# One sort key: VectorE forms the negated row maxima of a head group before the low part of a later group's queries

## The chip, the cores and the metric

One core of a Trainium2 chip. The metric is the device time of one execution in microseconds (us), as the median of several runs; less is better. Five engines work side by side: TensorE (PE, with its weight loads as PEld), VectorE (DVE), ScalarE (ACT), GpSimd (POOL) and SyncE (SP), which here only issues transfers. Each runs its own list of instructions in order and meets the others through semaphores.

## What is computed

An attention block (8 sequences of 512 tokens, 256 channels, 16 heads, latent width 32), a layer norm of input plus attention, a soft mixture of 16 experts, and a last layer norm. Only the attention matters here:

```
q_lat = rope(q @ q2l_w.T + q2l_b)      k_lat = rope(k @ kv2l_w.T + kv2l_b)
q_for_k = q_lat @ wqk_w.T + wqk_b
att = softmax(causal(q_for_k @ k_lat.T * 32 ** -0.5))
y = (att @ v_lat) @ l2o_w.T + l2o_b
```

## The kernel before

**Groups.** The 16 heads of a sequence are taken in four groups of four, so there are 32 groups over the 8 sequences; they are numbered 0 to 31 here (group 4b + g is group g of sequence b). The score matrix of a group is computed twice. A first pass of six "max" units (matmul lines 1461 and 1464) is reduced by VectorE to row maxima `mx` (line 1171). The negated maxima then become two more rows of the query operand `qks`, so that the second pass, six "exp" units (line 1477), comes out of TensorE already shifted and ScalarE only takes the exponential (line 874). GpSimd sets the causal part to zero (line 724, the "mask" steps) and TensorE multiplies with the values (line 1488).

**From maxima to rows (steps `negmax` and `neg`).** VectorE forms -mx in two small `scalar_tensor_tensor` instructions of 128x16: line 1179 writes the high part from `mx` and `zeros`, line 1181 the rest from `mx` and the high part, after a semaphore wait on the first. TensorE transposes the pair into the PSUM bank `misc` (line 1469), ScalarE copies it out (line 864) and a transfer on ScalarE's queue places it in `qks` (line 869).

**Queries (steps `wqk`, `qhi`, `qlo`, `stack`).** Two groups ahead, TensorE writes a group's queries into the same bank `misc` (line 1448). ScalarE rounds them to the high part (line 852) and VectorE forms the low part (line 1165, in from PSUM and from SBUF, 128x512). That instruction also hands `misc` back (`misc_drained`), and SyncE then issues twelve transfers that stack the group's operands in `qks` (line 411) for its max units.

```
elif name == "qlo":
    g = st[2]
    dve.wait_ge(q_high, group(b, g))
    nc.vector.scalar_tensor_tensor(out=stg[g % 2][:, 0, :], in0=misc[:, :], scalar=bwq[:, 0:1],
                                   in1=fp(stg[g % 2][:, 1, :]), op0=ALU.add, op1=ALU.subtract).then_inc(misc_drained, 1)
...
elif name in MISC_STEPS:
    pe.wait_ge(misc_drained, misc_count(st, 0))
...
elif name == "neg":
    g = st[2]
    pe.wait_ge(neg_ready, group(b, g))
```

TensorE's `misc` users follow one another in the order in which TensorE has them: queries of group n+2 (`wqk`), maxima of group n (`neg`), a transpose of outputs (`yT`). So the transpose of group n's maxima waits for two things of VectorE: the maxima themselves (`neg_ready`, line 1181) and the bank, which the low query part of group n+2 (line 1165) gives back.

**Rotary products.** GpSimd multiplies the rotated latents of a coming group by the sine (line 704, both inputs in SBUF, 128x1024) and adds the cosine product of VectorE (line 1161) to it (line 710).

**Order.** `order()` gives each step of an engine a time: 8 slots per group plus the offset of its kind in `PE_AT`, `DVE_AT` and so on (single steps of the first sequence have fixed times in `DVE_EARLY` and its likes), and sorts by it. In `DVE_AT`, `qlo` of group n+2 stands at 8(n+2) - 10.0 = 8n + 6.0, `negmax` of group n at 8n + 6.05, the first max unit of group n+1 at 8n + 4.89 and the second at 8n + 6.22.

Of the kernel before, what the change touches and what calls it, by code (L numbers as in the profile page):

```python
# [40 lines left out]

PE_AT = {"lat": -20.25, "wqk": -9.25, "max": 0.0, "neg": 11.0, "exp": 13.25, "v": 14.55, "pv": 15.75, "yT": 28.75, "yTT": 53.5, "cproj": 58.5, "wv": -10.384, "seT": 5.624}
ACT_AT = {"stack": -9.0, "xth": -30.5, "lat": -22.0, "khi": -12.85, "qhi": -9.58, "neg": 9.57, "exp": 11.74, "y": 22.25, "yTT": 52.85, "apply": 76.25, "wlat": -30.402, "senorm": -2.024, "seT": 7, "seh": 9.429}
DVE_AT = {"xtl": -32.0, "blat": -28.9, "kvrows": -28.8, "slotg": -28.781, "shuffle": -21.3, "cos": -17.25, "qlo": -10.0, "max": -3.11, "negmax": 6.05, "v": 11.5, "yT": 26.15, "cproj": 55.1, "ln": 56.75, "wlat": -30.314, "wv": -17.071, "sestat": -23.24, "sescale": -7.5, "sel": 9.985}
POOL_AT = {"sin": -26.06, "add": -23.69, "klo": -21.92, "mask": 2.69, "bias": 42.5}
SP_AT = {"xt": -52.5, "x": 28.5, "stack": -22.15, "store": 83.25}

# [111 lines left out]
def block_kernel(nc, a, out):  # L159
# [316 lines left out]
    with nc.Block() as block:  # L476
# [550 lines left out]
        def _(dve):  # L1027
# [46 lines left out]

            for st in order(DVE_AT, DVE_FRONT, DVE_LAST, DVE_JOIN, DVE_EARLY):
                name, b = st[:2]
# [623 lines left out]
```

## Time and profile before

| what | value |
|---|---|
| median of 3 runs | 1191.9 us (1191.51 to 1192.89) |
| profiled execution | 1193.62 us, of which the profile's span is 1191.9 us |
| mean granted clock of TensorE | 0.983 of full speed |
| busy, share of the span | PE 95%, PEld 76%, DVE 65%, ACT 56%, POOL 49% |
| chain that ended last, by engine | PE 83%, DVE 8%, ACT 5%, issue 2% |

The attention fills the span up to about 525 us. Busy time is the time in which an engine's instructions run; for TensorE they overlap, since they are pipelined. The chain that ended last is followed back from the last instruction, at each step to what released it. In a timeline, an instruction that waits inside the engine counts as running.

### The profile page before, as it was taken

What the parts mean: (1) busy time and instruction counts of PE and PEld (TensorE: products, weight loads), DVE (VectorE), ACT (ScalarE), POOL (GpSimd) and SP (SyncE); (2) the same over time, 40 slices, a digit from 0 to 9 for tenths busy, and PEclk for the clock granted to TensorE, in tenths of its full rate; (3) what the DMA queues carried; (4) which work ended last, traced back from release to release, by engine and by line L of the source; (5) the groups of instructions that cost most, each with busy time, mean ns of one, the idle gap of its engine ahead of it and who ended that gap; (6) DMA issues with size and microseconds to landing.
All of it is one profiled execution on the core that took longest, in us unless ns stands there. A gap on an engine that the chain in (4) does not pass through costs nothing.

```text
span 1191.9 us, 19111 instructions
## 1 busy us (share of the span) xinstructions
PE 1137.4 (95%) x6849; PEld 904.1 (76%) x6882; DVE 772.6 (65%) x1251; ACT 670.3 (56%) x946; POOL 579.4 (49%) x399
## 2 busy tenths in 40 slices
PE   7799999999999999997999999979999999999996
PEld 5566767676767667665888888858888888888885
DVE  6878787879696978656677777635455454523344
ACT  2555565665666565656797777745556555530112
POOL 5555565556556555421666666664444544430000
PEclk9899999999999999989999999999999999999998
DMA  4645454645455655611144335365555445365661
GB/s 150 146 106 140 114 124 107 162 113 155 114 157 123 160 126 127 171 61 53 60 160 159 125 124 185 100 202 176 167 179 185 146 152 165 115 216 170 242 224 54
DMA packets 126670, 170.29 MB, mean 143 GB/s; under 512 B 47041, under 2 KB 77186, under 8 KB 126594
## 3 DMA queue, kind: packets, MB, share of 16 engines
q1 hardware_dynamic: 124018, 167.95, 48.4%
q10 hardware_dynamic: 2576, 1.35, 0.5%
q8 instruction: 45, 0.74, 0.3%
q14 instruction: 31, 0.25, 0.1%
HBM read 72.26 MB, written 37.75 MB: 92 GB/s over the span
## 4 chain that ended last, share of the span: by engine, by line
PE 83%; DVE 8%; ACT 5%; issue 2%; POOL 1%; DMA 1%; SPq 1%; ACTq 0%; DVEq 0%; POOLq 0%
PE ring L456 12%; PE ring L457 11%; PE ring L458 11%; PE ring L1627 7%; PE tail L1488 6%; PE ring L1477 5%; PE ring L1461 4%; PE tail L456 4%; PE tail L458 4%; PE tail L457 4%; ACT pt L874 3%; PE ring L1510 2%; PE tail L1627 2%; PE tail L1448 2%; PE ring L1564 2%
## 5 line engine op out<-in xcount | busy, mean ns | idle before, releaser
L1171 DVE TENSOR_REDUCE mx<-ring 128x4 f32<-128x512 f32 (+2 forms) x192 | 199.7, 1042 | 72.8 <-PE ring L1464 55.5
L874 ACT ACTIVATE pt<-ring 128x1024 f32<-128x1024 f32 (+1 forms) x192 | 169.0, 881 | 91.6 <-PE ring L1477 87.6
L724 POOL TENSOR_SCALAR_AFFINE_SELECT pt<-pt 128x512 f32<-128x512 f32 x128 | 81.4, 636 | 187.9 <-ACT pt L874 187.9
L1477 PE MATMUL ring<-qks 98*128 98x256 f32 (+3 forms) x512 | 136.7, 370 | 4.5 <-DVE mx L1171 2.0
L1461 PE MATMUL ring<-qks 96*128 96x384 f32 (+3 forms) x512 | 120.1, 337 | 5.3 <-DMA qks<-stg 4.1
L741 POOL TENSOR_TENSOR dl<-e,dh 128x1024 fp32r<-128x1024 f32 x32 | 76.5, 2403 | 94.3 <-ACT e L945 94.3
L765 POOL TENSOR_TENSOR hl<-hid,hh 128x512 fp32r<-128x512 f32 x64 | 82.7, 1303 | 76.9 <-ACT hh L980 76.9
L1477 PEld LDWEIGHTS ring<-qks 98*128 98x128 f32 x512 | 79.3, 191 | 32.2 <-issue 20.5
L1289 DVE SCALAR_TENSOR_TENSOR hid<-ring,bias_e,gate 128x512 f32<-128x512 f32 x64 | 47.9, 748 | 81.1 <-ACT gate L974 49.5
L1461 PEld LDWEIGHTS ring<-qks 96*128 96x128 f32 x512 | 80.8, 193 | 20.5 <-issue 5.9
L710 POOL TENSOR_TENSOR rope<-rope,rot 128x1024 f32<-128x1024 f32 x31 | 75.1, 2421 | 36.5 <-DVE rope L1161 36.5
L1627 PE MATMUL ring<-eo,c 128*128 (+1 forms) x384 | 88.3, 379 | 0.0
L1488 PE MATMUL tail<-pt,va 128*32 128x512 f32 (+3 forms) x1024 | 83.0, 440 | 0.0
L974 ACT ACTIVATE gate<-ring,bias_e 128x512 f32<-128x512 f32 x64 | 44.1, 689 | 67.4 <-PE ring L458 61.4
L1627 PEld LDWEIGHTS ring<-eo,c 128*128 128x128 f32 x384 | 72.9, 190 | 9.9
L757 POOL TENSOR_TENSOR wul<-wu,wuh 128x1024 fp32r<-128x1024 f32 x16 | 42.5, 2657 | 76.0 <-ACT wuh L799 76.0
L1014 ACT ACTIVATE y<-y,nmr,r 128x256 f32<-128x256 f32 x32 | 16.7, 590 | 104.6 <-DVE nmr L1354 104.6
L704 POOL TENSOR_TENSOR rot<-rot,sin 128x1024 f32<-128x1024 f32 x31 | 73.8, 2382 | 1.3 <-DVE rot L1145 1.1
L817 ACT ACTIVATE lat<-ring,blat 128x512 f32<-128x512 f32 x32 | 22.1, 690 | 90.9 <-PE ring L458 73.1
L980 ACT ACTIVATE hh<-hid 128x512 fp32r<-128x512 f32 x64 | 40.2, 628 | 58.2 <-PE tail L458 49.2
L456 PE MATMUL tail<-wdh,hh 128*128 128x256 f32 x240 | 67.9, 283 | 0.5 <-POOL hl L765 0.5
L458 PE MATMUL tail<-wdl,hh 128*128 128x256 f32 x240 | 67.9, 283 | 0.0
(247 smaller groups left out, 3071.6 us busy)
## 6 DMA issues: line engine op xcount, KB each, us to landing
qks<-stg SPq DMA_DIRECT2D x378, 128.0 KB, 2.5
c_dram<-c2s SPq DMA_DIRECT2D x32, 512.0 KB, 5.0
c<-c_dram SPq DMA_DIRECT2D x32, 512.0 KB, 6.6
sl_dram<-sls SPq DMA_DIRECT2D x32, 256.0 KB, 3.4
wg<-in_wg SPq DMA_DIRECT2D x16, 512.0 KB, 5.4
wu<-in_wu SPq DMA_DIRECT2D x16, 512.0 KB, 6.3
wd<-in_wd SPq DMA_DIRECT2D x16, 512.0 KB, 7.1
sl<-sl_dram SPq DMA_DIRECT2D x16, 512.0 KB, 4.5
```

The lines of the kernel that those rows point to most:

```text
L456: nc.tensor.matmul(dst, lh, rh, start=first, stop=False)
L457: nc.tensor.matmul(dst, ll, rh, start=False, stop=False)
L458: return nc.tensor.matmul(dst, lh, rl, start=False, stop=last)
L724: nc.gpsimd.affine_select(out=m, in_=m, compare_op=ALU.is_ge, fill=0.0, base=0, pattern=[[0, GH], [1, P]], channel_multiplier=-1).then_inc ...
L741: nc.gpsimd.tensor_tensor(out=dl[h][:, rows, :], in0=e2[u][:, :, :], in1=fp(dh[h][:, rows, :]), op=ALU.subtract).then_inc(d_low, 1)
L765: nc.gpsimd.tensor_tensor(out=hl[:, f, :], in0=hid[f % 2][:, :], in1=fp(hh[:, f, :]), op=ALU.subtract).then_inc(hid_low, 1)
L874: nc.scalar.activation(pt[j][:, h:h + heads, 0:n], heads_of(tile, heads, n), ACT.Exp, scale=SCALE).then_inc(empty, 1)
L1171: nc.vector.tensor_reduce(out=mx[:, g, h:h + heads, i], in_=heads_of(tile, heads, (i + 1) * P), axis=AX.X, op=ALU.max).then_inc(empty, 1)
L1461: nc.tensor.matmul(scores[:, h, :], qks[0:KS_ROWS, g, 0, h0 + h, i * P:(i + 1) * P], qks[0:KS_ROWS, g, 1, h0 + h, 0:n], start=(h % some == ...
L1477: last = nc.tensor.matmul(scores[:, h, :], qks[0:KS_ROWS + 2, g, 1, h0 + h, j * P:(j + 1) * P], qks[0:KS_ROWS + 2, g, 0, h0 + h, j * P:T], ...
L1488: last = nc.tensor.matmul(ybank[h * L:(h + 1) * L, j * P:T], va[:, j, g * GH + h, :], pt[j][:, h, 0:T - j * P], start=(j == 0), stop=(j == ...
L1627: last = nc.tensor.matmul(acc[i][t // 2][:, t % 2, 0:DO], c2[i][:, n, t * P:(t + 1) * P], eo[:, n, b, :], start=(n == 0), stop=(n == NS - 1))
```

## The change

VectorE's offset for `qlo` goes from -10.0 to -9.9. The low query part of group n+2 then has the time 8n + 6.1 and stands behind the negated maxima of group n (8n + 6.05) and still ahead of the second max unit of group n+1 (8n + 6.22). No other step lies between, and no other engine's order changes. The steps of groups 0 to 2 have fixed times, so 29 pairs of neighbours are swapped: maxima of groups 1 to 29, low query parts of groups 3 to 31.

```
-DVE_AT = {... "cos": -17.25, "qlo": -10.0, "max": -3.11, "negmax": 6.05, ...
+DVE_AT = {... "cos": -17.25, "qlo": -9.9, "max": -3.11, "negmax": 6.05, ...
```

## Rows read from the trace of the kernel before

**Rows 1.** Stretches: us, busy per engine (instructions), TensorE clock, DMA share, GB/s.

```profile
281.00:343.00 62.00, 61.18 (x420) 43.33 (x424) 50.97 (x82) 38.76 (x59) 36.30 (x29) 1.00 0.55 137
```

**Rows 2.** Timeline, all engines, around group 17: start us, length us, engine, line.

```profile
308.17 2.38 POOL L704 TENSOR_TENSOR rot<-rot,sin 128x1024 f32<-128x1024 f32 x1
...
308.90 0.69 DVE L1171 TENSOR_REDUCE mx<-ring 128x4 f32<-128x512 f32 x1 [0.54 <-remote]
308.99 0.68 ACT L852 ACTIVATE stg<-tail,bwq 128x512 fp32r<-128x512 f32 x1
...
309.70 0.75 DVE L1165 SCALAR_TENSOR_TENSOR stg<-tail,bwq,stg 128x512 fp32r<-128x512 f32 x1
...
310.37 0.22 DVE L1179 SCALAR_TENSOR_TENSOR negmax<-mx,zeros 128x16 fp32r<-128x16 f32 x1
...
310.51 0.63 POOL L724 TENSOR_SCALAR_AFFINE_SELECT pt<-pt 128x512 f32<-128x512 f32 x1
...
310.62 0.55 DVE L1181 SCALAR_TENSOR_TENSOR negmax<-mx,negmax 128x16 fp32r<-128x16 f32 x1
...
310.88 0.28 PE L1464 MATMUL ring<-maskb,identb 128*128 128x128 bf16 x2
311.10 1.21 DVE L1171 TENSOR_REDUCE mx<-ring 128x4 f32<-128x1024 f32 x1
...
311.32 0.27 PE L1469 MATMUL tail<-ident,negmax 128*32 128x128 f32 x1 [0.15 <-DVE negmax L1181]
```

**Rows 3.** TensorE's waits, whole execution: who waited for whom, us, times, longest.

```profile
PE tail L1469 <- DVE negmax L1181: 3.9, 22, 0.4
```

**Rows 4.** Timeline around group 0, where no query part precedes the maxima.

```profile
49.73 2.38 POOL L704 TENSOR_TENSOR rot<-rot,sin 128x1024 f32<-128x1024 f32 x1
...
51.28 0.85 DVE L1179 SCALAR_TENSOR_TENSOR negmax<-mx,zeros 128x16 fp32r<-128x16 f32 x1
...
52.17 0.17 DVE L1181 SCALAR_TENSOR_TENSOR negmax<-mx,negmax 128x16 fp32r<-128x16 f32 x1
...
52.49 0.27 PE L1469 MATMUL tail<-ident,negmax 128*32 128x128 f32 x1 [0.40 <-DVE negmax L1181]
```

**Rows 5.** Timeline around group 30, whose maxima no query part precedes either.

```profile
507.09 0.17 DVE L1179 SCALAR_TENSOR_TENSOR negmax<-mx,zeros 128x16 fp32r<-128x16 f32 x1
...
507.29 0.17 DVE L1181 SCALAR_TENSOR_TENSOR negmax<-mx,negmax 128x16 fp32r<-128x16 f32 x1
...
508.06 0.64 POOL L724 TENSOR_SCALAR_AFFINE_SELECT pt<-pt 128x512 f32<-128x512 f32 x1 [3.51 <-ACT pt L874]
```

**Rows 6.** The low query part over the whole execution: ns min/median/max.

```profile
L1165 DVE SCALAR_TENSOR_TENSOR stg<-tail,bwq,stg x32: 722/751/760, 25.8 to 493.8; 128x512 fp32r<-128x512 f32 x32
```

**Rows 7.** Timeline around group 6, third of its sequence.

```profile
139.45 0.55 DVE L1181 SCALAR_TENSOR_TENSOR negmax<-mx,negmax 128x16 fp32r<-128x16 f32 x1
...
143.06 0.29 PE L1464 MATMUL ring<-maskb,identb 128*128 128x128 bf16 x2
143.19 0.27 PE L1469 MATMUL tail<-ident,negmax 128*32 128x128 f32 x1
...
144.60 2.39 POOL L710 TENSOR_TENSOR rope<-rope,rot 128x1024 f32<-128x1024 f32 x1
...
146.27 0.74 DVE L1208 TENSOR_SCALAR nv<-meanvar 128x4 f32<-128x4 f32 x1
```

**Rows 8.** Timeline around group 1, TensorE.

```profile
67.33 0.29 PE L1464 MATMUL ring<-maskb,identb 128*128 128x128 bf16 x2
...
67.77 0.27 PE L1469 MATMUL tail<-ident,negmax 128*32 128x128 f32 x1
```

**Rows 9.** Timeline, stacking of group 5 and its first max unit.

```profile
94.01 8.88 SPq L411 DMA_DIRECT2D qks<-stg  x12
...
105.32 0.56 PE L1461 MATMUL ring<-qks 96*128 96x128 f32 x4
```

**Rows 10.** Page, DMA issues: count, KB each, median us from issue to landing.

```profile
qks<-stg SPq DMA_DIRECT2D x378, 128.0 KB, 2.5
```

## What the change will do, foretold from the trace of before

> **What bounds the kernel now.** I read the stretches first, to see whether the attention is bound by one engine; then the waits of TensorE; then the timeline of one group; then the same instructions in groups where something around them differs.
>
> Over one sequence in the steady part TensorE is busy for 61.18 of 62 us at full granted clock, VectorE for 51 [rows 1]. So whatever keeps TensorE idle there is added to the time, and little idle time is left in which a new stall could be given back. The waits of TensorE name the place of the change: the transpose of the negated maxima waited 22 times for line 1181, 3.9 us in all [rows 3]. One of the 22 is group 0, with 0.40 us [rows 4], whose order the change leaves alone. So 21 of the 29 swapped groups have VectorE's maxima on the path. The other eight are groups 6, 10, 14, 18, 22 and 26, where TensorE comes to the transpose 3.2 us after the maxima are there (139.45 + 0.55 = 140.00 against 143.19, [rows 7]), and groups 1 and 29, where line 1181 ends just as TensorE gets there.
>
> In group 17 VectorE does: max unit (to 309.59), low query part 309.70 to 310.45, line 1179 310.37 to 310.59, line 1181 310.62 to 311.17, next max unit; the transpose starts 0.15 later, at 311.32 [rows 2]. What the reader is to see is the length of the two small instructions. Both handle 128x16, yet take 0.22 and 0.55 us. In group 30 they take 0.17 each [rows 5]. The difference is GpSimd: in group 17 line 1179 ends 0.04 us after GpSimd's sine product (308.17 + 2.38 = 310.55), line 1181 0.03 us after GpSimd's mask (310.51 + 0.63 = 311.14) [rows 2]; in group 30 GpSimd does nothing until 508.06 [rows 5]. Groups 2 to 28 all show the pattern of group 17, 27 times over. Group 0 is the test, since it has no query part in front of the maxima: line 1179 begins while the sine product runs, takes 0.85 us and ends at 52.13, 0.02 after the product (49.73 + 2.38 = 52.11); line 1181, with no mask behind the product, takes 0.17 [rows 4]. So a small instruction with both inputs in SBUF stands still until the GpSimd instruction under way ends, whenever it came. The low query part, one input of which is in PSUM, takes 722 to 760 ns in all 32 groups [rows 6], the sine product beside it or not.
>
> **The change part by part.** It adds and removes no instruction; 29 times it exchanges 0.75 us of work with a pair of small instructions.
>
> The maxima first. Each instruction of VectorE starts 0.07 to 0.08 us before the end of the one in front (310.37 against 310.45, [rows 2]). Behind the max unit, line 1179 would start so at 309.51 in group 17. The sine product runs until 310.55, so line 1179 ends at 310.59 as before, now after 1.08 us instead of 0.22. The mask follows the product as before, so line 1181 ends at 311.17 as before. The maxima gain nothing.
>
> The query part next. ScalarE's high part is there at 309.67 (308.99 + 0.68, [rows 2]), so nothing but VectorE's order holds line 1165. It starts 0.07 before line 1181's end, as the next max unit did (311.10 against 311.17), and ends at 311.10 + 0.75 = 311.85. In effect the query part used to run in the shadow of the sine product, and the shadow is now spent on waiting.
>
> The transpose waits for the bank as well as for the maxima, so its releaser becomes line 1165: 311.85 + 0.15 = 312.00 instead of 311.32, 0.67 to 0.68 us more. I take 0.67. On VectorE the next max unit and the cosine product are queued behind; they move by the same 0.67, and TensorE, which has to drain them later, has moved with them. TensorE, ScalarE and GpSimd then go on from the transpose as before, all shifted, and the next group repeats it: the phase between the sine product, which hangs on an exponential and so on TensorE, and the max unit stays.
>
> Bounds for a group: below, the pair of small instructions costs 0.37 us from first start to last end, as in group 30 (507.09 to 507.46, [rows 5]); then the query part ends at 309.51 + 0.37 - 0.07 + 0.75 = 310.56, the transpose is released at 310.71, and TensorE, which without a wait starts it 0.13 after line 1464 (143.06 and 143.19, [rows 7]), goes at 310.88 + 0.13 = 311.01, a gain of 0.31. Above, both wait in full: 0.67. I take the upper end, because group 0 is the changed order with the sine product running [rows 4].
>
> The Trainium skill, "VectorE: DVE Perf Modes", section on the TRN2 errata, gives an fp32 two-input instruction of N elements (N + 151) / 0.96 ns, an estimate of 0.174 us for 16 elements: the 0.17 of group 30 agrees, the 0.22 and 0.55 of group 17 don't. By that figure alone the sum would be a gain of about 7 us. The Trainium skill, "SBUF — State Buffer", section "Who interferes with whom", says that a VectorE instruction with two SBUF inputs and a GpSimd instruction that reads SBUF exclude each other, the later one waiting for the earlier one's end: by that rule the sum is the loss below, and groups 0 and 17 agree with it.
>
> The other eight swapped groups. Six don't wait at the transpose. There VectorE runs late instead, by at most 0.67, until line 1208 in the layer norm, which already takes 0.74 us and ends at 147.01, with GpSimd's addition (144.60 + 2.39 = 146.99, [rows 7]): the lag ends in that wait, so 0; without that cover six such lags would reach TensorE, at most 6 x 0.44 = 2.6 us (0.67 less some 0.2 that VectorE idles ahead of the layer norm). In groups 1 and 29 no sine product is running when line 1179 comes. There the transpose gains 67.77 - (67.33 + 0.13) = 0.31 each [rows 8]. Together -0.6.
>
> The stacking. Its twelve transfers follow line 1165, so they start 1.40 us later, of which TensorE's own shift takes back 0.67. The tightest place is group 5's stack: the last of twelve issues starts about 0.6 us before 94.01 + 8.88 = 102.89, lands about 2.5 us later [rows 10], so near 104.8, and its first max unit runs at 105.32 [rows 9]. A slack of 0.5 against 0.73: at most 0.2 us, once. Elsewhere it is 1.3 us or more. I cost it at nothing.
>
> Sum: 21 x 0.67 = 14.1, less 0.6, is +13.5 us. On the profiled execution (1193.62 us, of which 1191.9 in the span) that is 1207.1; on the median of the runs shown, 1191.9, it is 1205.4.
>
> **The rivals.**
> *Nothing holds the maxima* (0.07). If line 1179 doesn't wait for a product that was running long before, 21 + 2 groups gain 0.31: -7.1 us, 1184.8. It decides if line 1179 takes about 0.2 us in groups 2 to 28. Group 0 speaks against it.
> *Half of the wait* (0.09). Line 1179, ready early, is through at the product's end and line 1181 gets ahead of the mask (310.62 to 310.79): the query part ends at 310.72 + 0.75 = 311.47, the transpose starts at 311.62, +0.30 in 21 groups, less 0.6: +5.7, 1197.6. Against it: in group 17 line 1179 was already waiting at the product's end, and the mask still went first [rows 2].
> *Given back* (0.05). TensorE has 62 - 61.18 = 0.8 us idle per sequence [rows 1], and seven sequences of it would not cover 13.5 us. Still, if the lists absorb the shift, it is within 0.2%, 1191 to 1193.
> *More than the sum* (0.05). Lags in the six groups and a late stack: 13.5 + 2.6 + 0.2, 1208.2.
> The forecast holds 0.74, with its own range of 1203.5 to 1207.
>
> **How the numbers follow.** 0.2% of the time, 2.4 us, is about what a measurement can tell from no change. Faster 0.07, same 0.05, slower 0.74 + 0.09 + 0.05 = 0.88. The range runs from below the half wait (1197) to the sum with all lags (1208.5) and leaves out the first and third rival, 0.12.
>
> **What the profile of the changed kernel would show.** Line 1179 at about 1.1 us instead of 0.23 in groups 2 to 28, ending with the sine product; line 1181 still 0.55, ending with the mask; line 1165 behind them at 0.75; the transpose waiting for line 1165 and no longer for line 1181, idle about 0.67 us more each time; the steady sequence 62.0 + 3 x 0.67 = 64.0 us long. The prediction is wrong if line 1179 comes out short, if the mask falls behind line 1181, or if the sequence is longer by less than 2 us.

## The result, and the profile of the changed kernel

The changed kernel takes 1201.64 us (median of 6 runs, 1200.84 to 1204.66) against 1191.57 us of the kernel before (6 runs, 1189.51 to 1192.89). The ratio is 1.0085, with a 95% interval of 1.0072 to 1.0098: slower by 10.1 us, 8.6 to 11.7. The forecast was 1205.4 us, in a range of 1197.0 to 1208.5. Direction and mechanism were right; the size came out 3.8 us too large, below the likeliest case's own range (1203.5 to 1207).

The profiled execution's span is 1200.6 us. Around group 17 its timeline reads, against [rows 2] of the kernel before (start us, length us, engine, line):

```profile
314.41 2.39 POOL L704 TENSOR_TENSOR rot<-rot,sin 128x1024 f32<-128x1024 f32 x1
...
315.14 0.69 DVE L1171 TENSOR_REDUCE mx<-ring 128x4 f32<-128x512 f32 x1 [0.54 <-PE ring L1464]
315.22 0.68 ACT L852 ACTIVATE stg<-tail,bwq 128x512 fp32r<-128x512 f32 x1
...
315.75 1.07 DVE L1179 SCALAR_TENSOR_TENSOR negmax<-mx,zeros 128x16 fp32r<-128x16 f32 x1
...
316.74 0.64 POOL L724 TENSOR_SCALAR_AFFINE_SELECT pt<-pt 128x512 f32<-128x512 f32 x1
...
316.86 0.55 DVE L1181 SCALAR_TENSOR_TENSOR negmax<-mx,negmax 128x16 fp32r<-128x16 f32 x1
...
317.12 0.29 PE L1464 MATMUL ring<-maskb,identb 128*128 128x128 bf16 x2
317.33 0.74 DVE L1165 SCALAR_TENSOR_TENSOR stg<-tail,bwq,stg 128x512 fp32r<-128x512 f32 x1
...
317.99 1.21 DVE L1171 TENSOR_REDUCE mx<-ring 128x4 f32<-128x1024 f32 x1
318.10 0.59 SPq L411 DMA_DIRECT2D qks<-stg  x1
...
318.13 0.28 PE L1469 MATMUL tail<-ident,negmax 128*32 128x128 f32 x1 [0.73 <-DVE stg L1165]
```

Line 1179 now follows the max unit at once, but has GpSimd's sine product beside it, which ends at 314.41 + 2.39 = 316.80. It takes 1.07 us instead of 0.22 and ends at 316.82. Line 1181 ends at 317.41, behind the mask (316.74 + 0.64 = 317.38). Only then does VectorE come to the low query part, 0.74 us, which used to run while the sine product ran. TensorE needs its end for the bank `misc`: the transpose has stood idle for 0.73 us, and its releaser is line 1165.

TensorE's waits for VectorE at the transpose, over the whole execution, read, against [rows 3] (us in all, times, longest):

```profile
PE tail L1469 <- DVE stg L1165: 15.3, 21, 0.7
...
PE tail L1469 <- DVE negmax L1181: 0.4, 1, 0.4
```

So 21 groups wait for the query part, the 21 that waited for line 1181 before. The one wait left for line 1181 is group 0's. The three VectorE lines over the whole execution (ns, shortest/median/longest) show that group 17 is the rule:

```profile
L1179 DVE SCALAR_TENSOR_TENSOR negmax<-mx,zeros x32: 165/1074/1094, 50.8 to 532.1; 128x16 fp32r<-128x16 f32 x32
...
L1181 DVE SCALAR_TENSOR_TENSOR negmax<-mx,negmax x32: 174/549/566, 51.7 to 532.3; 128x16 fp32r<-128x16 f32 x32
...
L1165 DVE SCALAR_TENSOR_TENSOR stg<-tail,bwq,stg x32: 734/739/764, 25.3 to 505.4; 128x512 fp32r<-128x512 f32 x32
```

Line 1179's median goes from 0.228 to 1.074 us; the other two stay (549 against 550 ns, 739 against 751). And a stretch of 62 us in the steady part (us, busy per engine, clock, DMA share, GB/s) reads, against [rows 1]:

```profile
281.00:343.00 62.00, 59.56 (x405) 42.34 (x403) 51.84 (x79) 37.87 (x58) 35.02 (x29) 1.00 0.51 127
```

TensorE's granted clock is 1.00 as before; it is busy for 59.56 us instead of 61.18 because it stands still, not because it runs slower.

**Where the time lies.** The starts of the transposes measure it group by group. Here are those of groups 1, 21 and 28 after the change:

```profile
66.95 0.27 PE L1469 MATMUL tail<-ident,negmax 128*32 128x128 f32 x1
...
381.86 0.28 PE L1469 MATMUL tail<-ident,negmax 128*32 128x128 f32 x1 [0.72 <-DVE stg L1165]
...
492.34 0.28 PE L1469 MATMUL tail<-ident,negmax 128*32 128x128 f32 x1 [0.73 <-DVE stg L1165]
```

And those of groups 21 and 28 in the kernel before:

```profile
373.36 0.27 PE L1469 MATMUL tail<-ident,negmax 128*32 128x128 f32 x1 [0.16 <-DVE negmax L1181]
...
480.90 0.27 PE L1469 MATMUL tail<-ident,negmax 128*32 128x128 f32 x1 [0.18 <-DVE negmax L1181]
```

From group 1 to group 28 it was 480.90 - 67.77 [rows 8] = 413.13 us; now it is 492.34 - 66.95 = 425.39, 12.26 more. A second profiled execution of the changed kernel (below) has 11.67 more. Group by group the step from the transpose before to the group's own grew by 0.53 to 0.62 us in the 21 waiting groups and by -0.01 to 0.09 in the six others; groups 1 and 29 gained 0.32 and 0.22. From group 17 to group 21, one sequence, it was 373.36 - 311.32 [rows 2] = 62.04 us and is 381.86 - 318.13 = 63.73.

### The profile page after: what moved, and what is told of

The parts are those of the page before. It is cut to its first block, busy times and chain, and to the rows that moved or that the text cites. A ratio compares the mean times of both kernels' runs of the same rounds, so it can differ in the third digit from the quotient of the medians.

```text
span 1200.6 us, 19144 instructions
## 1 busy us (share of the span) xinstructions
PE 1134.5 (94%) x6882; PEld 900.9 (75%) x6882; DVE 788.3 (66%) x1251; ACT 669.8 (56%) x946; POOL 579.9 (48%) x399
## 4 chain that ended last, share of the span: by engine, by line
PE 83%; DVE 9%; issue 3%; DMA 2%; SPq 1%; ACT 1%; POOL 1%; ACTq 0%; DVEq 0%; POOLq 0%
PE ring L456 12%; PE ring L457 11%; PE ring L458 11%; PE ring L1627 7%; PE tail L1488 6%; PE ring L1477 5%; PE ring L1461 5%; PE tail L456 4%; PE tail L457 4%; PE tail L458 4%; PE ring L1510 2%; PE tail L1627 2%; PE tail L1448 2%; DVE negmax L1179 2%; PE ring L1464 2%
```

## Experiments

Two theories. *Standstill*: the loss is the time in which line 1179, and then line 1181, stand still beside GpSimd, which now passes on to the low query part and the bank. *Order*: the loss comes with the later query part itself, through its later stack or the later bank, whether GpSimd holds the maxima or not.

**Maxima that need not stand still, in both orders.** Both small instructions become reductions with one SBUF input; line 1180 (a copy of zeros) then stands in place of line 1181.

```diff
-blink(nc.vector.scalar_tensor_tensor(out=negmax[:, g, 0, :, :].bitcast(f32r), in0=mx[:, g, :, :], scalar=-1.0,
-                                     in1=zeros[:, :, :], op0=ALU.mult, op1=ALU.add))
-nc.vector.scalar_tensor_tensor(out=negmax[:, g, 1, :, :].bitcast(f32r), in0=mx[:, g, :, :], ...
+blink(nc.vector.tensor_reduce(out=negmax[:, g, 0, :, :], in_=mx[:, g, :, :].unsqueeze(3), axis=AX.X, op=ALU.max, negate=True))
+nc.vector.tensor_reduce(out=negmax[:, g, 1, :, :], in_=zeros[:, :, :].unsqueeze(3), axis=AX.X, op=ALU.max).then_inc(neg_ready, 1)
```

> The changed order (maxima in front of the query part), but both small instructions are reductions over a last axis of length one with a single SBUF input: the first writes the negated maximum, the second copies zeros, so the low part of the maxima is left out (a softmax's shift need not be exact). Standstill theory (a small instruction with two SBUF inputs stands still until the GpSimd instruction under way ends): nothing stands still any more, line 1179 and its partner take 0.2 us each, the query part ends 0.65 us before where line 1181 ended in the kernel before, the transpose starts without a wait, 0.31 us earlier in 21 + 2 groups: 1191.6 - 7 = about 1184.5 us, ratio to before 0.994. Rival one (the small instructions wait for the max unit in front of them or for their semaphores, whatever their inputs): they stay at about 1.07 and 0.55 us and the time stays at about 1201.6. Rival two (the loss comes from the stacking transfers, which start later behind the query part): the stack still starts later than before by about 0.1 us only, so this run alone can't tell it from the standstill.

> The order of before (query part in front), with the same one-input instructions (low part of the maxima left out). Standstill theory: line 1181 ends near 310.77 instead of 311.17 in group 17, below the 311.01 at which TensorE can start, so the gain is the same 0.31 us in 21 + 2 groups as in the changed order: about 1184.5 us, and the two orders differ by less than 1 us, since the order only matters through the standstill. Rival one: 1191.6, as before, and 10 us away from the changed order with the same instructions.

Measured beside 1191.16 us of the kernel before: new order 1184.97 (ratio 0.9944, 0.9924 to 0.9964), old order 1184.96 (0.9943, 0.9925 to 0.9961). Once the two instructions need not stand still, the order makes no difference that these runs can tell, and none near 10 us. In the new order, group 17:

```profile
304.14 2.38 POOL L704 TENSOR_TENSOR rot<-rot,sin 128x1024 f32<-128x1024 f32 x1
...
305.48 0.16 DVE L1179 TENSOR_REDUCE negmax<-mx 128x16 f32<-128x16 f32 x1
305.67 0.17 DVE L1180 TENSOR_REDUCE negmax<-zeros 128x16 f32<-128x16 f32 x1
...
305.76 0.74 DVE L1165 SCALAR_TENSOR_TENSOR stg<-tail,bwq,stg 128x512 fp32r<-128x512 f32 x1
...
306.85 0.28 PE L1462 MATMUL ring<-maskb,identb 128*128 128x128 bf16 x2
...
306.97 0.27 PE L1467 MATMUL tail<-ident,negmax 128*32 128x128 f32 x1
```

The sine product runs until 306.52, and both small instructions pass beside it in 0.16 and 0.17 us. The query part ends at 306.50, before TensorE is there, and the transpose (line 1467 here) waits for nothing. *Order* falls: all of the loss hangs on the standstill. It is not the operation either: line 1165 is a `scalar_tensor_tensor` too, with one input in PSUM, and is not held [rows 6].

**The sine product behind the mask.** The second way to take away what makes line 1179 wait: the product starts later, behind the group's second mask.

```diff
-POOL_AT = {"sin": -26.06, "add": -23.69, ...
+POOL_AT = {"sin": -25.0, "add": -23.69, ...
```

> The changed order with the two-input instructions as they are; GpSimd's sine product (line 704) goes behind the second mask of a group instead of in front of it (its offset in POOL_AT from -26.06 to -25.0), so that no GpSimd instruction runs when the small ones come. Standstill theory: lines 1179 and 1181 take 0.17 us each, the transpose starts without a wait; the cosine product of VectorE (line 1161, two SBUF inputs) now meets the sine product and stands still for up to 1.2 us, which VectorE's idle time later in the group covers: 1184.5 to 1188 us. Rival one (max unit or semaphores): line 1179 stays near 1.07 us and the time near 1201.6. Should VectorE's slack not cover the cosine product's standstill, the time can reach 1195 while line 1179 is still at 0.17: then the length of line 1179 decides, not the time.

1198.13 us (1.0052, 1.0037 to 1.0068): the time was missed. Line 1179 did become short (median 168 ns), and the transpose's wait is gone, but another took its place. Around group 17, behind the transpose:

```profile
313.77 2.37 POOL L704 TENSOR_TENSOR rot<-rot,sin 128x1024 f32<-128x1024 f32 x1
...
314.27 2.95 DVE L1161 TENSOR_TENSOR rope<-lat,cos 128x1024 f32<-128x1024 f32 x1
...
316.10 1.62 POOL L724 TENSOR_SCALAR_AFFINE_SELECT pt<-pt 128x512 f32<-128x512 f32 x1
```

Now VectorE's cosine product, also with two SBUF inputs, meets the sine product: its median is 2.95 us, against 1.21 before. The max units behind it are late, and the waits of TensorE (45 to 535 us) say so:

```profile
PE ring L1477 <- DVE mx L1171: 14.6, 16, 1.4
```

In the same window of the kernel before, that wait was 2.0 us in 3 times. The overlap was not removed, it was moved to a dearer instruction.

**The sine product earlier.** The same line, the other way.

```diff
+POOL_AT = {"sin": -28.1, "add": -23.69, ...
```

> The changed order with the two-input instructions as they are; GpSimd's sine product goes in front of the first mask of a group (its offset from -26.06 to -28.1), so that it is over, or nearly, when the small ones come, and does not meet the cosine product as it did behind the second mask. Standstill theory: in most groups lines 1179 and 1181 take 0.17 us; in groups where VectorE's shuffle ends just ahead of that mask, the sine product and the first mask still hold them for some 0.3 and 0.6 us, without reaching the transpose. The transpose has no wait, the cosine product is back at 1.21 us: 1184 to 1188 us. Rival (order alone): near 1201.6. If GpSimd's first mask, now later, makes the product with the values wait (line 1488 for line 724), the time lies above 1188, and that wait shows it.

1189.17 us against 1192.32 of before (0.9972, 0.9959 to 0.9985): faster than both kernels, yet above the forecast of 1184 to 1188, because the product is often not through when the maxima come. Group 3:

```profile
90.18 2.38 POOL L704 TENSOR_TENSOR rot<-rot,sin 128x1024 f32<-128x1024 f32 x1 [1.83 <-ACT pt L874]
...
92.19 0.40 DVE L1179 SCALAR_TENSOR_TENSOR negmax<-mx,zeros 128x16 fp32r<-128x16 f32 x1
92.52 1.29 POOL L724 TENSOR_SCALAR_AFFINE_SELECT pt<-pt 128x512 f32<-128x512 f32 x2
92.62 0.55 DVE L1181 SCALAR_TENSOR_TENSOR negmax<-mx,negmax 128x16 fp32r<-128x16 f32 x1
93.10 0.74 DVE L1165 SCALAR_TENSOR_TENSOR stg<-tail,bwq,stg 128x512 fp32r<-128x512 f32 x1
```

Over all groups line 1179 has a median of 227 ns and line 1181 of 176, with the longest at 619 and 553. In place of the 21 waits of 15.3 us for line 1165 there are 6 of 1.5. TensorE's weight loads for the transpose, which this row does not count, wait for it more often (45 to 495 us):

```profile
PEld tail L1469 <- DVE stg L1165: 4.4, 14, 0.4
```

Group by group, against the one-input kernel in the new order: where lines 1179 and 1181 take 0.17 us each (groups 5, 9, 13, 17, 21 and 25), the step to the transpose is the same within 0.02 us; in the 15 others of the 21 groups, where one or both are held, it is 0.21 to 0.48 us longer, 5.1 us in all. So what is still paid is the standstill again. The sign named for the mask stays small: line 1488's weight loads wait for line 724 for 1.3 us in 8 times.

**Only line 1179 in front of the query part.** The changed kernel, but with line 1181 behind the query part (`query_low` holds line 1165; `blink` is the semaphore step and wait that now stand apart).

```diff
-blink(nc.vector.scalar_tensor_tensor(out=negmax[:, g, 0, :, :] ...))
+chain[0] += 1
+nc.vector.scalar_tensor_tensor(out=negmax[:, g, 0, :, :] ...).then_inc(dve_chain, 1)
+n = group(b, g, 2)
+if 3 <= n < B * G:
+    query_low(n // G, n % G)
+dve.wait_ge(dve_chain, chain[0])
 nc.vector.scalar_tensor_tensor(out=negmax[:, g, 1, :, :] ...
```

> The changed order with the query part (line 1165 of the kernel before) put between the two small instructions: first part of the maxima, query part of group n+2, rest of the maxima, all with two SBUF inputs as they were. Standstill theory: the first small instruction stands still until the sine product ends (about 1.07 us long), the query part runs beside GpSimd's mask, and the rest of the maxima comes after the mask has ended, so it takes 0.17 us instead of 0.55. From the end of the sine product to the transpose: 0.03 - 0.07 + 0.74 + 0.09 + 0.15 = 0.94 us, against 0.77 before and 1.34 with the change as made: +0.17 in 21 groups, less 0.6, about +3, near 1194.5 us; some two thirds of the loss go although the query part still stands behind the first small instruction. Rival (the order alone costs: each small instruction in front of the query part delays it by a fixed length): the rest of the maxima still takes 0.55 us, and the transpose comes at least as late as with the change as made, near 1201.6 us.

1195.13 us (1.0022, 1.0013 to 1.0032); group 17:

```profile
310.45 2.38 POOL L704 TENSOR_TENSOR rot<-rot,sin 128x1024 f32<-128x1024 f32 x1
...
311.79 1.07 DVE L1183 SCALAR_TENSOR_TENSOR negmax<-mx,zeros 128x16 fp32r<-128x16 f32 x1
...
312.78 0.74 DVE L1077 SCALAR_TENSOR_TENSOR stg<-tail,bwq,stg 128x512 fp32r<-128x512 f32 x1
312.79 0.63 POOL L724 TENSOR_SCALAR_AFFINE_SELECT pt<-pt 128x512 f32<-128x512 f32 x1
...
313.44 0.16 DVE L1189 SCALAR_TENSOR_TENSOR negmax<-mx,negmax 128x16 fp32r<-128x16 f32 x1
...
313.75 0.27 PE L1477 MATMUL tail<-ident,negmax 128*32 128x128 f32 x1 [0.31 <-DVE negmax L1189]
```

The first small instruction still pays 1.07 us for the sine product. The query part then covers the mask, and the second one takes 0.16. The transpose is 0.15 us later per waiting group than before, instead of 0.57. So the 0.57 splits: 0.42 of it comes from keeping the query part back until the mask is through as well, and 0.15 is left when it is kept back for the sine product alone, runs beside the mask and has line 1181 behind it.

**A later stack alone.** The kernel before, with the twelve transfers of group n+2 held back until the maxima of group n are formed.

```diff
+if group(b, g, 0) >= 3:
+    sp.wait_ge(neg_ready, group(b, g, 0) - 1)
```

> The kernel before, in its own order, but SyncE also waits for the negated maxima (line 1181) of the group two back before it issues a group's twelve stacking transfers, for all groups from number 3 on. That starts them about 0.72 us later against TensorE, which is what the change does to them (1.40 later, less TensorE's own shift of 0.57 to 0.67). Bank theory (the loss is the transpose's wait for the bank that the query part gives back): no change, 1191.6, within 0.2%. Rival two (the loss is the late stack): most of the 10 us, about 1198 to 1202.

The stack of group 19 then starts with the transpose of group 17, both at 311.83 us, as in the changed kernel (318.10 and 318.13); in the kernel before it starts at 310.48, 0.84 us ahead.

1194.33 us against 1191.16 (1.0017, 1.0005 to 1.0028): by the ratio +2.0 us, 0.6 to 3.3, by the medians +3.2; that is something, but far from most of the 10 us. TensorE's waits for the stack (line 1463 here, line 1461 in the others) show it:

```profile
PE ring L1463 <- DMA qks<-stg: 6.1, 5, 2.5
```

In the kernel before and in the changed one this row reads 4.1 us in 2 times, in their second profiles (below) 3.3 and 3.8. So a later stack can cost something, but the changed kernel's loss is not this: its 21 steps grow evenly, and its transposes wait for line 1165.

**No small instructions.** The experiments point to a version without them: in the old order, the max units write negated maxima at once (the low part is left at zero), and the transpose waits for the max units.

```diff
-nc.vector.tensor_reduce(out=mx[:, g, h:h + heads, i], ..., op=ALU.max).then_inc(empty, 1)
+nc.vector.tensor_reduce(out=negmax[:, g, 0, h:h + heads, i], ..., op=ALU.max, negate=True).then_inc(empty, 1)
```

> The order of before without any step for the maxima: each max unit writes its negated maxima straight into the rows that are transposed (a reduction with a negated result), the low part stays zero from the start (it is left out, the softmax's shift need not be exact), and the transpose waits for the max units themselves. VectorE loses 0.4 us per group, and nothing with two SBUF inputs is left at that place. Standstill theory: the transpose has no wait, as with the one-input instructions, so the same time, 1184.97 us within 2 us: VectorE's 13 us less of work are off the path. If VectorE's time itself mattered there (the rival that the lag of its later max units holds TensorE), it would come out 3 us or more below that.

> The kernel without small instructions once more, on the same chip as the next one (the low part of the maxima is left out in both). If VectorE's 0.4 us less per group matter beyond the standstill, it comes out 3 us below the next one, as in the earlier runs (1181.8 against 1185.0). The steady part of the two profiles (groups 1 to 28) differed by 0.1 us only, which speaks for the same time within 1.5 us and for a difference between chips or executions.

> The changed order with one-input instructions once more, beside the one above: the same time as that one within 1.5 us if only the standstill counts, 3 us more if VectorE's time counts as well.

1181.83 us against 1192.32 (0.9918, 0.9901 to 0.9935), and again 1180.71 against 1191.77 (0.9908, 0.9892 to 0.9923). It beats both kernels, as long as the low part of the maxima is not needed. Both forecasts for the standstill alone, the same time as with one input within 2 us and within 1.5 us, are missed. The one-input version of the new order, run beside it, took 1184.69 (0.9937, 0.9923 to 0.9950). From group 1 to 28 the two gain the same against the first profile of before, 6.77 and 6.84 us. So the 4.0 us between them lie outside the steady part. In this pair, 2.51 of the 3.6 us between the profiled spans lie between the transposes of groups 29 and 30 (15.62 against 18.13 us), a stretch that the next runs take up; in the pair run earlier, 2.1 of 3.0 us lie ahead of group 0's. What makes them stays open.

**Both kernels profiled once more.**

> The changed kernel, a second profile. The sum by groups: from the transpose of group 1 to that of group 28 again 12.3 us more than before (21 x 0.58), and about 0.3 less at groups 1 and 29. Open is the stretch from group 29 to group 30, which no swap touches between: 15.7 us in the first profile against 17.8 before. If that is a matter of one execution (how fast the stack of group 31 lands), it comes out anywhere between 15.5 and 20.5; if the change shortens it, near 15.7 again.

> The kernel before, a second profile, for the same question: groups 1 to 28 again in 413.1 us within 0.5; the stretch from group 29 to group 30 anywhere between 15.5 and 20.5 us if it is a matter of one execution, 17.8 if not.

1200.94 us (span 1199.2) and 1190.11 us (span 1188.4), a pair of spans 10.8 us apart, against 8.7 for the first pair. From group 1 to group 28 the kernel before takes 412.91 us (413.13 in its first profile) and the changed one 424.80, 11.89 more, a little less than expected; 20 of its groups wait for line 1165 instead of 21. The pairs differ above all in one stretch: from the transpose of group 29 to that of group 30 the kernel before needs 17.84 us in its first profile and 15.30 in its second, the changed one 15.71 and 15.76. The first profile of before, first TensorE's wait for the stack of group 31, then the clock in the stretch that follows:

```profile
505.45 0.63 PE L1461 MATMUL ring<-qks 96*128 96x128 f32 x4 [1.74 <-DMA qks<-stg]
```

```profile
505.00:507.00 2.00, 1.55 (x7) 1.49 (x9) 0.52 (x1) 0.00 (x0) 0.00 (x0) 0.77 0.83 213
507.00:509.00 2.00, 2.00 (x9) 1.70 (x8) 1.00 (x4) 0.81 (x1) 0.64 (x1) 0.50 1.03 422
509.00:511.00 2.00, 2.00 (x10) 1.69 (x9) 0.65 (x1) 0.00 (x0) 0.00 (x0) 0.88 0.31 125
```

The second profile, wait and clock over the same time:

```profile
503.81 0.63 PE L1461 MATMUL ring<-qks 96*128 96x128 f32 x4 [0.81 <-DMA qks<-stg]
```

```profile
505.00:507.00 2.00, 2.00 (x14) 1.79 (x13) 1.88 (x4) 0.81 (x1) 0.64 (x1) 1.00 0.98 395
507.00:509.00 2.00, 2.00 (x12) 1.77 (x10) 0.00 (x0) 0.00 (x0) 0.00 (x0) 1.00 0.49 201
```

In the first profile TensorE stood without work for 1.74 us, and its granted clock then fell to 0.50 (1.2 instead of 2.4 GHz); in the second it stood for 0.81 us, and the clock stayed at 1.00. The sum fits: 0.93 us more wait, and 2 x (0.23 + 0.50 + 0.12) = 1.7 us of clock (some 3.4 us at 0.50), make 2.6, near the 2.54 seen. The kernel before shows both within its own two profiles, so this belongs to one execution and not to the change. In the nine other runs the stretch takes 15.62 to 20.30 us, long and short ones with the new order, and its longest value is with the old one.

## Why the prediction was right, and where it was off

- **The maxima gain nothing.** Forecast: line 1179 at 1.08 us, ending with the sine product, line 1181 at 0.55, ending with the mask. Measured 1.07 and 0.55, ends 0.02 and 0.03 us behind GpSimd's. Group 0 [rows 4] was the right place to read the changed order from. That the standstill is the cause is shown by the one-input runs: take it away, and the order is worth nothing. The Trainium skill, "SBUF — State Buffer", section "Who interferes with whom", adds that a reduction never contends with GpSimd on this chip; both reductions of 128x16 took 157 to 171 ns in all 32 groups of the new order, sine product beside them or not, so this case agrees. The prediction's other page, "VectorE: DVE Perf Modes" of the Trainium skill, gives its formula for an fp32 tensor_tensor; that it fits these small instructions too is shown by group 30's 0.17 us alone.
- **The query part behind them, and the transpose behind it.** Right in kind: releaser line 1165, 21 groups, and the query part, covered before, uncovered now.
- **The size of a group's step: the term that was off.** The prediction took 0.67 us, from 311.85 + 0.15 = 312.00 against 311.32. Line 1165 ended about as foreseen, 0.66 us behind line 1181 (318.07 against 317.41; foreseen 0.68). But the 0.15 was measured behind line 1181, whose result the transpose reads (311.17 to 311.32, [rows 2]). Behind line 1165, which only gives the bank back, the transpose starts 318.13 - 318.07 = 0.06 after the end; in all 21 groups it is 0.05 or 0.06, against 0.14 or 0.15 before. The step is 0.66 - 0.15 + 0.06 = 0.57, and 21 x 0.57 = 12.0 us instead of 14.1. The latency was carried over from one producer to another without a row for the new one, and the bounds given for a group did not name it. The run with line 1181 last again supports it: there the gap is 313.75 - 313.60 = 0.15.
- **The prediction's own test.** It said it would be wrong if a sequence grew by less than 2 us. It grew by 1.69, three times 0.56: by its own words the prediction fails that test, and the same term is the reason. Its other signs, line 1179's length and the mask ahead of line 1181, came as said.
- **The six groups with cover.** Forecast 0, measured -0.01 to 0.09 each. The lag ends in line 1208's wait as said: in group 6 that line takes 0.34 us instead of 0.74 and still ends 0.01 us behind GpSimd's addition; over the seven from 45 to 535 us its mean is 323 ns, against 660 before.
- **Groups 1 and 29.** Forecast a gain of 0.31 each, measured 0.32 and 0.22.
- **The stack.** Forecast nothing; TensorE's wait for it is 4.1 us in the first profiles of both kernels.
- **The sum.** 21 x 0.57 + 6 x 0.04 - 0.54 = 11.7; the transposes give 12.26 - 0.54 = 11.7 in the first profile. The medians differ by 10.1, 8.6 to 11.7. What lies between, up to 1.6 us, is outside the groups and less than the 2.54 us by which the two profiles of the kernel before differ at group 31's stack; whether the changed order shortens that part systematically stays open.
- **The rivals.** *Nothing holds the maxima* falls with line 1179's 1.07 us. Its price was good, though: it worked out 7.1 us less for maxima that nothing holds, and the one-input runs, where nothing does, took 6.2 us less, 1184.97 and 1184.96. *Half of the wait* falls because the mask still goes ahead of line 1181 (316.74 against 316.86). *Given back* falls with the interval. *More than the sum* falls with the six groups and the stack.

## What to carry to other kernels

Before moving a small instruction that reads two SBUF operands, look at what GpSimd does at its new place: its price is the rest of the GpSimd instruction under way, and whatever stood in that shadow before has to be paid behind it. Better than moving it is to make it a reduction with one SBUF input, or to do without it (negate in the max units): that was worth 0.6% here as a reduction, in either order, and 0.8 to 0.9% without, against the 0.85% that the order alone lost. Both versions leave the low part of the maxima out. One SBUF input alone is not enough: line 1208, a `tensor_scalar` with a single input, 128x4, stands still as well (next section). And when the releaser of a wait changes, take the gap from its end to the consumer's start from a row with that producer.

## What the runs showed of the hardware

- The standstill goes both ways. VectorE's cosine product, issued 0.5 us behind GpSimd's sine product, took 2.95 us instead of 1.21, and the mask that GpSimd issued at 316.10, while that product ran, took 1.62 instead of 0.63: sine product, cosine product and mask ended one behind the other, at 316.14, 317.22 and 317.72.
- An instruction with one SBUF input can stand still too. Line 1208 (`tensor_scalar`) took 0.74 us in group 6 and ended 0.02 us behind GpSimd's addition [rows 7]. Where GpSimd had nothing under way, in the kernel before, it took 0.17:

```profile
516.33 0.17 DVE L1208 TENSOR_SCALAR nv<-meanvar 128x4 f32<-128x4 f32 x1
```

- From the end of a VectorE instruction to the start of the TensorE instruction that waits for it there are two lengths, and the size of the VectorE instruction does not sort them. Here, in the kernel before, is one of 128x1024 with 0.14 us behind it (566.77 to 566.91), and a max unit, which reads as much, with 0.06 (402.54 to 402.60):

```profile
565.55 1.22 DVE L1225 TENSOR_TENSOR xnl<-xn,xnh 128x1024 fp32r<-128x1024 f32 x1
...
566.91 0.77 PE L456 MATMUL tail<-seh,xnh 128*128 128x512 f32 x1 [3.67 <-DVE xnl L1225]
```

```profile
401.32 1.22 DVE L1171 TENSOR_REDUCE mx<-ring 128x2 f32<-128x1024 f32 x1
...
402.60 0.62 PE L1477 MATMUL ring<-qks 98*128 98x384 f32 x2 [0.16 <-DVE mx L1171]
```

  In all the traces it is 0.14 to 0.16 us where TensorE waits for data that VectorE makes (lines 1181, 1191, 1225, 1248), and 0.05 to 0.07 where it only waits for a PSUM bank to be given back (lines 1165, 1171, 1087), in every row up to 580 us that shows the VectorE instruction by itself. Why there are two lengths is not shown.
